# One consecutive block of 98 nodes per partition in the prologue of a graph-network kernel

## The chip, the cores and the metric

The kernel runs on one core of one Trainium2 chip. The metric is the device time of one execution in microseconds (us); the time before is 3852.42 us, the median of three runs (3849.85 to 3852.91).

## The reference

One layer of a message-passing network with 12,500 nodes of 128 features and 400,000 edges, which arrive sorted by their destination. All arithmetic is float32.

```python
h = jnp.maximum(_layernorm(x, axis=-1), 0.0)          # 12500 x 128, no scale or shift
m = relu(concat([h[src], h[dst], ea]) @ w1 + b1) @ w2 + b2      # 400000 x 128, ea has 32 columns
agg = segment_sum(m, dst, num_segments=12500)
gi = agg @ w_ih + b_ih ; gh = h @ w_hh + b_hh         # 3 gates of 128
r = sigmoid(i_r + h_r) ; z = sigmoid(i_z + h_z) ; n = tanh(i_n + r * h_n)
out = x + (1.0 - z) * n + z * h
```

## The kernel before

**Prologue.** The nodes are padded to 12,544 = 98 tiles of 128 (`NT`), and handled in 14 batches of 7 tiles (`NB`), alternately with parity 0 and 1. Node `n*128 + p` lies on partition `p` of tile `n`. For each batch SyncE loads x into `acc` (`load_x`, L313), VectorE takes the statistics (L805, L811), ScalarE the square root (`deviation`, L556), VectorE the reciprocal and the shift (`scales`, L820, L822). The normalising is shared: VectorE has tiles 0 and 1 (L830), GpSimd tiles 2 to 5 (L473, L475), ScalarE tile 6 (L565). TensorE transposes the seven tiles into PSUM (L1121). ScalarE applies the ReLU twice from the same PSUM: into `hT_batch` (L575), which TensorE reads as weights for the products with `w1_src` (L1130), and into `hT` (L576), the table of features by nodes that is kept for the whole kernel. ScalarE copies the products to `stage` (L583), and SyncE stores them in DRAM as `p_rows` (`store`, L319), row `n` of which is the product of node `n`. `stage`, the PSUM areas and `xn` have two buffers each, one for each parity. Each engine's program is in order; SyncE, TensorE, VectorE and ScalarE run the middle batches in a hardware loop of two batches a turn.

**Between.** SyncE loads the destinations in four parts into `dst_nat` (125 rows, L361), among the last stores. VectorE reduces them to the least and greatest node of each of the 125 chunks and two sets (L862, L863), and makes the window bases (`ranges_ready`) and the violations, which say whether the fast way is allowed. ScalarE makes `w2ih` and `b2ih` with TensorE (L619 to L623), then writes the bases to DRAM and reads them back, one copy for its registers and one on all partitions (L626 to L630), then zeroes two thirds of `acc` (L633); VectorE zeroes the rest (L878), makes `node_at` (L884), sets ones in `lhs` (L885), copies the iota to PSUM (L887) and makes the flag (L1103, L1104). Every engine waits for the flag before it goes on (`choose`, L303).

**Chunks.** The edges are handled in 125 chunks of 5 groups (`G`) of 5 tiles (`T`) of 128 edges. Per chunk GpSimd issues 24 indirect DMAs, each of which gathers 128 rows of `p_rows` (L501, `rows`). The 25th tile, tile 4 of group 3 (`PICKED`), is not gathered: for its 128 edges ScalarE (96) and VectorE (32) copy columns of `hT` into `picked` (L667, L938), a quarter in each of the steps 0 to 3, at node numbers that they read from `low` (`pick_act`, `pick_dve`), and TensorE multiplies (L1192). For the other groups TensorE computes the part from the destination and the edge features (L1187), VectorE adds it to the gathered rows (L947), ScalarE applies the ReLU (L673), and TensorE sums by destination with a one-hot matrix (L1207, `seg_ready`). The gathers of group `s` of the next chunk wait for `seg_ready[s]`. GpSimd starts the gathers of chunk 0 once all of `p_rows` is stored, before the flag. SyncE loads three groups ahead (`AHEAD`). For the picks it loads the node numbers of all chunks in two DMAs (L422), after the first three groups' loads and after the zeroes of `acc` were copied to `deg`.

Of the kernel before, what the change touches and what calls it, by code (L numbers as in the profile page):

```python
# [18 lines left out]
NB = 7  # L19
LOADS_AHEAD = 4  # L20
N_ZERO_DVE = N // 3

POOL_FROM = 2
ACT_FROM = 6
BATCHES = NT // NB
TAIL = N - (NT - 1) * P
# [8 lines left out]
CHUNKS = GROUPS // G  # L35
TILES = GROUPS * T
# [24 lines left out]
PICKS_DVE = (8, 8, 8, 8, 0)  # L61
PICKS_ACT = (24, 24, 24, 24, 0)
N_DVE, N_ACT = sum(PICKS_DVE), sum(PICKS_ACT)
assert N_DVE + N_ACT == P
# [12 lines left out]
def gnn_kernel(nc, x, src_cols, dst_cols, dst_rows, src_tiles, dst_tiles, ea_t, w1, b1, w2, b2, w_ih, b_ih, w_hh, b_hh, out):  # L77
# [7 lines left out]
    with ExitStack() as ctx:  # L85
# [6 lines left out]
        def sems(name, n):  # L92
# [5 lines left out]
        hT = sb("hT", [P, NPAD])  # L98
        low = sb("low", [P, NPAD])
# [17 lines left out]
        hT_batch = [low[:, at + k * NB * D:at + (k + 1) * NB * D] for k in range(2)]  # L117
        at += 2 * NB * D
# [5 lines left out]
        pick_dve = low[2 * ED:2 * ED + 1, 0:CHUNKS * N_DVE].bitcast(I32)  # L124
        pick_act = low[3 * ED:3 * ED + 1, 0:CHUNKS * N_ACT].bitcast(I32)
# [33 lines left out]
        zero_col = sb("zero_col", [P, 1])  # L159
# [52 lines left out]
        violT_ps = ps[0:1, 4096 - P:4096 - P + CHUNKS]  # L212
# [9 lines left out]
        pad_zeroed, x_tail_in = sem("pad_zeroed"), sem("x_tail_in")  # L222
# [3 lines left out]
        scaled, xn_dve_ready, xn_pool_ready, xn_act_ready, xT_ready, hT_ready, hT_kept = (sems(n, 2) for n in (  # L226
            "scaled", "xn_dve_ready", "xn_pool_ready", "xn_act_ready", "xT_ready", "hT_ready", "hT_kept"))
# [13 lines left out]
        pick_in, picked_dve, picked_act = (sem(n) for n in ("pick_in", "picked_dve", "picked_act"))  # L241
# [4 lines left out]
        g_src_in, g_dst_in = (sem(n) for n in ("g_src_in", "g_dst_in"))  # L246
        g_gathered = sems("g_gathered", 3)
# [62 lines left out]
        def _(sp):  # L310
            def load_x(k, par):
                xv = x[0:(NT - 1) * P, :].rearrange("(n p) f -> p n f", p=P)
                sp.dma_start(xt[:, bass.ds(k * NB, NB), :], xv[:, bass.ds(k * NB, NB), :]).then_inc(x_in[par], 16)  # L313

            pv = p_rows.rearrange("(n p) f -> p n f", p=P)
# [17 lines left out]
            sp.wait_ge(pad_zeroed, 1)  # L333
            sp.dma_start(xt[0:TAIL, NT - 1, :], x[(NT - 1) * P:N, :]).then_inc(x_tail_in, 16)
# [9 lines left out]
            k = BATCHES - 1  # L344
            sp.wait_ge(x_in[1], k // 2 * 16)
            xv = x[0:(NT - 1) * P, :].rearrange("(n p) f -> p n f", p=P)
# [8 lines left out]
            for s in range(G):  # L355
                load_indices(0, s)
# [1012 lines left out]
```

## Time and profile before

| | us |
|---|---|
| median of three runs | 3852.42 |
| the profiled execution's own time | 3851.74 |
| its span, first to last instruction | 3850.0 |
| GpSimd busy | 2863.6 (74%) |
| TensorE busy, matmul / weight load | 2907.2 (76%) / 2648.2 (69%) |
| VectorE busy | 2077.9 (54%) |
| ScalarE busy | 1921.0 (50%) |

The first 110 us are the prologue and the preparation of the chunks, the rest is the chunk loop, whose 40 slices on the page look alike. Issuing a DMA is not counted as busy, with the exception of GpSimd's indirect DMAs, which have rows of their own. The granted clock of TensorE is 1.0 of full speed in the prologue's loop, 0.5 between 64 and 100 us, and 0.74 over the whole span.

### The profile page before, as it was taken

The page shows a single profiled execution, that of the slowest core. Times are in us where ns is not written, and L with a number is a line of the kernel's source. Part 1 is how long each engine was busy: PE and PEld are TensorE (multiplying, and loading weights), DVE is VectorE, ACT ScalarE, POOL GpSimd, SP SyncE. Part 2 cuts the span into 40 slices and gives each one's busy share as a digit, 9 for nine tenths or more (in the row PEclk, how much of TensorE's full clock was granted, in tenths as well). Part 3 has the DMA queues.
Part 4 walks back from the last instruction along what each step waited for, and adds up shares of the span by engine and source line. Part 5 has one row for each costly group of instructions (what it writes and reads, how often), then busy time and mean ns, then how long its engine had stood idle before and what let it go on. Part 6 is the DMA issues. An engine that isn't in the chain of part 4 may idle for free.

```text
span 3850.0 us, 94115 instructions
## 1 busy us (share of the span) xinstructions
PE 2907.2 (76%) x16157; PEld 2648.2 (69%) x16157; DVE 2077.9 (54%) x8517; ACT 1921.0 (50%) x13700; POOL 2863.6 (74%) x3039
## 2 busy tenths in 40 slices
PE   4777777777678777877777777777777777787777
PEld 4677677667677766776766676677667767677776
DVE  5555555555555555555555555555555555555554
ACT  5545554455544455455544555445554455545553
POOL 5677777777777777777777777777777777777775
PEclk8777777877876677677777767777777776767776
DMA  7444444444444444444444444444444444444443
GB/s 187 111 113 111 111 111 111 115 111 111 111 112 112 111 111 111 112 111 111 111 111 112 111 111 111 111 114 112 111 111 111 112 111 111 111 112 111 111 111 80
DMA packets 439603, 433.42 MB, mean 113 GB/s; under 512 B 180055, under 2 KB 331062, under 8 KB 439572
## 3 DMA queue, kind: packets, MB, share of 16 engines
q0 software_dynamic: 96000, 196.80, 22.4%
q1 hardware_dynamic: 315254, 223.36, 19.5%
q10 hardware_dynamic: 28318, 12.94, 1.2%
q14 instruction: 23, 0.19, 0.0%
q8 instruction: 8, 0.13, 0.0%
HBM read 419.89 MB, written 12.82 MB: 112 GB/s over the span
## 4 chain that ended last, share of the span: by engine, by line
POOL 51%; issue 23%; PE 14%; DMA 3%; ACT 2%; ACTq 2%; DVE 1%; POOLq 1%; DVEq 0%; SPq 0%
POOL rows L501 51%; PE ps L1207 6%; DMA rows<-p_rows,idx 3%; ACT picked L667 2%; ACTq L658 2%; PE ps L1187 2%; PE ps L1222 2%; PE ps L1224 1%; PE ps L1221 1%; DVE rows L947 1%; PE ps L1192 1%; PE ps L1225 1%; POOLq L257 0%; POOLq L285 0%; DVE low L959 0%
## 5 line engine op out<-in xcount | busy, mean ns | idle before, releaser
L501 POOL DMA_INDIRECT rows<-p_rows,idx x3000 | 2833.2, 944 | 940.7 <-issue 897.8
L667 ACT COPY picked<-hT 128x1 f32 x12000 | 1181.4, 187 | 552.9 <-issue 552.9
L1187 PE MATMUL ps<-rhs,lhs 128*128 128x128 f32 x6250 | 1108.8, 341 | 72.5 <-DVE rows L947 67.5
L1207 PE MATMUL ps<-onehot,rows 128*128 128x95 f32 x6250 | 1074.4, 336 | 116.5 <-DVE low L959 116.5
L1207 PEld LDWEIGHTS ps<-onehot,rows 128*128 128x128 f32 x6250 | 1034.4, 253 | 153.7 <-issue 153.7
L947 DVE TENSOR_TENSOR rows<-rows,ps 128x640 f32<-128x640 f32 x625 | 495.7, 793 | 1153.9 <-DMA rows<-p_rows,idx 1146.9
L1187 PEld LDWEIGHTS ps<-rhs,lhs 128*128 128x128 f32 x6250 | 1020.8, 251 | 104.1 <-DVE rows L947 70.0
L673 ACT ACTIVATE rows<-rows 128x640 f32<-128x640 f32 x625 | 447.1, 715 | 1215.2 <-DVE rows L947 1213.8
L915 DVE TENSOR_SCALAR_CACHE_REDUCE lhs<-dst_row,node_at 95x640 f32<-95x640 int32 x625 | 543.3, 869 | 5.1 <-DMA dst_row<-in_dst_rows_dram 5.1
L906 DVE TENSOR_TENSOR onehot<-dst_rel,ps 128x475 f32<-128x475 f32 x625 | 401.0, 642 | 0.0
L938 DVE COPY picked<-hT 128x1 f32 x4000 | 349.8, 146 | 7.7 <-issue 7.7
L958 DVE TENSOR_TENSOR acc<-acc,ps 128x95 f32 x250 | 63.6, 254 | 511.9 <-PE ps L1210 441.7
L1192 PE MATMUL ps<-w_keep,picked 128*128 128x128 f32 x250 | 72.6, 381 | 339.8 <-ACT picked L667 339.8
L1229 PE MATMUL ps<-ident,upd 128*100 128x128 f32 x123 | 44.2, 359 | 336.9 <-DVE upd L978 336.9
L1192 PEld LDWEIGHTS ps<-w_keep,picked 128*128 128x128 f32 x250 | 46.8, 234 | 361.7 <-issue 361.7
L1222 PE MATMUL ps<-low,b2ih 1*128 (+1 forms) x738 | 267.4, 462 | 0.0
L1229 PEld LDWEIGHTS ps<-ident,upd 128*100 128x100 f32 x123 | 16.9, 137 | 363.4 <-DVE upd L978 362.9
L1221 PE MATMUL ps<-acc,w2ih 128*128 (+1 forms) x738 | 225.4, 407 | 0.0
L1222 PEld LDWEIGHTS ps<-low,b2ih 1*128 1x128 f32 x738 | 177.8, 298 | 62.8 <-issue 59.4
L1221 PEld LDWEIGHTS ps<-acc,w2ih 128*128 128x128 f32 x738 | 191.5, 317 | 0.0
L1224 PE MATMUL ps<-hT,whh_sb 128*128 (+1 forms) x492 | 180.7, 470 | 0.0
L1224 PEld LDWEIGHTS ps<-hT,whh_sb 128*128 128x128 f32 x492 | 120.7, 304 | 42.4 <-issue 40.6
(101 smaller groups left out, 1364.4 us busy)
## 6 DMA issues: line engine op xcount, KB each, us to landing
dst_row<-in_dst_rows_dram SPq DMA_DIRECT2D x625, 240.0 KB, 3.8
lhs<-in_ea_t_dram SPq DMA_DIRECT2D x625, 80.0 KB
rows<-p_rows,idx POOLq DMA_INDIRECT x3000
idx<-in_src_cols_dram SPq DMA_DIRECT2D x625, 2.5 KB
p_rows<-low SPq DMA_DIRECT2D x14, 448.0 KB, 4.4
x_fin<-in_x_dram ACTq DMA_DIRECT2D x123, 50.0 KB
out_dram<-out_fin ACTq DMA_DIRECT2D x123, 50.0 KB
acc<-in_x_dram SPq DMA_DIRECT2D x13, 448.0 KB, 4.5
```

Of the source, the lines that this page charges most:

```text
L501: pool.indirect_dma_start(out=rows[:, s, t, :], out_offset=None, in_=p_rows[:, :], in_offset=bass.IndirectOffsetOnAxis(ap=idx[:, s, t:t + ...
L667: last = nc.scalar.copy(picked[:, e:e + 1], hT[:, bass.ds(node, 1)])
L673: nc.scalar.activation(m, m, ACT.Relu).then_inc(message_ready[s], 1)
L906: nc.vector.tensor_tensor(onehot[:, ONEHOT_PLACE[s], :, 0:W], dst_rel[:, s * T:(s + 1) * T].unsqueeze(2).to_broadcast([P, T, W]), iota_ps. ...
L915: nc.vector.tensor_scalar(lhs[0:W, s, :, 0:P], dst_row[0:W, s, :].rearrange("w (t p) -> w t p", t=T), node_at[0:W, bass.ds(c * NSETS + SET ...
L938: last = nc.vector.tensor_copy(picked[:, e:e + 1], hT[:, bass.ds(node, 1)])
L947: nc.vector.tensor_tensor(r, r, pre_ps[s % 2][:, 0:k * D], ALU.add).then_inc(summed[s], 1)
L1187: last = nc.tensor.matmul(pre_ps[s % 2][:, t * D:(t + 1) * D], lhs[:, s, t, 0:P], rhs[:, k, :], start=True, stop=gathered)
L1207: done = nc.tensor.matmul(sg[:, 0:W], rows[:, s, t, :], onehot[:, ONEHOT_PLACE[s], t, 0:W], start=(first and t == 0), stop=(last and t == ...
L1221: nc.tensor.matmul(gate_ps[:, g, :], w2ih[:, cols], a, start=True, stop=False)
L1222: last = nc.tensor.matmul(gate_ps[:, g, :], b2ih[0:1, cols], d, start=False, stop=(g == 2))
L1224: nc.tensor.matmul(gate_ps[:, g, :], whh_sb[:, cols], h, start=False, stop=True)
```

## The change

- x is padded with zero rows to 12,544, and partition `p` now holds nodes `98*p` to `98*p + 97`: `load_x` and `store` move 7 consecutive rows of 512 bytes per partition, one piece of 3584 bytes, where there were seven pieces. The load of the last rows and the zeroing of the pad are gone.
- The transposed tile `n` now holds nodes `98*p + n`, so `hT`, still in node order, is written and read as weights at a step of 98 columns (`hT_nodes`). `hT_batch` and the ReLU into it are gone; the products read `hT_nodes`.
- The normalising is shared anew: VectorE 1 tile, GpSimd 4, ScalarE 2.
- TensorE's loop over the middle batches is unrolled.
- The destinations are loaded after the last store, whole rows in two parts (112 and 13 rows). VectorE zeroes all of `acc` before it reduces them. The flag is made directly after the violations, ahead of `w2ih` on TensorE and ahead of `node_at` on VectorE. ScalarE issues the DMAs of the bases before `w2T`, `w2ih` and `b2ih`. The ones in `lhs` are set at VectorE's very start.
- The node numbers of the picks are loaded for one step at a time (`load_picks`, four small DMAs per chunk, three steps ahead), and those of chunk 0 ahead of the wait for the zeroes of `acc`. ScalarE and VectorE wait for each (`wait_picks`), before the ReLU or the sum of the step.

```diff
-POOL_FROM = 2
-ACT_FROM = 6
+POOL_FROM = 1
+ACT_FROM = 5
+EVEN = CHUNKS // 16 * 16
+        hT_nodes = hT[:, :].rearrange("f (p n) -> f n p", n=NT)
-        hT_batch = [low[:, at + k * NB * D:at + (k + 1) * NB * D] for k in range(2)]
             def load_x(k, par):
-                xv = x[0:(NT - 1) * P, :].rearrange("(n p) f -> p n f", p=P)
+                xv = x.rearrange("(p n) f -> p n f", p=P)
-            pv = p_rows.rearrange("(n p) f -> p n f", p=P)
+            pv = p_rows.rearrange("(p n) f -> p n f", p=P)
...
-            store(turns + 0, 0)
-            load_ranges(0)
-            load_ranges(1)
             store(turns + 0, 1)
...
+            store(turns + 3, 1)
+
+            for first, last in ((0, EVEN), (EVEN, CHUNKS)):
+                sp.dma_start(dst_nat[first:last, :], dst_rows[first:last, :]).then_inc(dstn_in, 16)
+            sp.dma_start(w1_dst[:], w1[D:2 * D, :]).then_inc(weights_in, 16)
...
+            def load_picks(c, s):
+
+                wait(sp, picked_act, (c - 1) * len(TURN_PICKS) + s + 1)
+                wait(sp, picked_dve, (c - 1) * len(TURN_PICKS) + s + 1)
+                first, n = TURN_PICKS[s]
+                sp.dma_start(picks[:, first:first + n], nodes_of[bass.ds(c, 1), first:first + n]).then_inc(pick_in[s], 16)
...
                 for s in range(AHEAD):
                     load_group(0, s)
+                for s in range(len(TURN_PICKS)):
+                    load_picks(0, s)
...
-            def relu_tiles(i, par, first):
+            def relu_tiles(i, par):
                 act.wait_ge(xT_ready[par], i + 1)
-                if not first:
-                    act.wait_ge(p_ready[par], i)
-                nc.scalar.activation(hT_batch[par], xT_ps[par], ACT.Relu).then_inc(hT_ready[par], 1)
-                nc.scalar.activation(hT[:, bass.ds((i * 2 + par) * (NB * D), NB * D)], xT_ps[par], ACT.Relu).then_inc(hT_kept[par], 1)
+                nc.scalar.activation(hT_nodes[:, bass.ds((i * 2 + par) * NB, NB), :], xT_ps[par].rearrange("f (n p) -> f n p", p=P), ACT.Relu).then_inc(hT_kept[par], 1)
...
+            act.wait_ge(ranges_ready, 1)
+            act.dma_start(base_f_dram, base_f[0:CHUNKS, :]).then_inc(base_stored, 16)
+            act.dma_start(base_i_dram, base_n[0:CHUNKS, :]).then_inc(base_stored, 16)
             act.wait_ge(w2T_ready, 1)
             nc.scalar.copy(w2T, setup_ps[:, 0:D]).then_inc(w2T_copied, 1)
+            act.wait_ge(base_stored, 32)
...
-            nc.scalar.copy(acc[:, N_ZERO_DVE:N], zero_col[:].to_broadcast([P, N - N_ZERO_DVE])).then_inc(acc_zeroed, 1)
...
+            nc.vector.memset(acc[:, 0:N], 0.0).then_inc(acc_zeroed, 1)
...
+            dve.wait_ge(dstn_in, 32)
...
+            dve.wait_ge(violT_ready, 1)
+            link(nc.vector.tensor_reduce(flag_f[:], violT_ps, AX.X, ALU.max))
+            nc.vector.tensor_scalar(flag_i[:], flag_f[:], 0.0, None, ALU.is_gt).then_inc(flag_ready, 1)
+
             dve.wait_ge(base_bc_in, 16)
...
-                    last = nc.tensor.matmul(p_ps[par][:, t * D:(t + 1) * D], hT_batch[par][:, t * D:(t + 1) * D], w1_src,
+                    last = nc.tensor.matmul(p_ps[par][:, t * D:(t + 1) * D], hT_nodes[:, (i * 2 + par) * NB + t, :], w1_src,
                                             start=True, stop=True)
...
-            with pe.Fori(1, BATCHES // 2 - 1) as i:
+            for i in range(1, BATCHES // 2 - 1):
```

## Rows read from the trace of the kernel before

**Rows 1.** Costliest groups of the page: busy and mean ns; idle before, and releaser.

```profile
L501 POOL DMA_INDIRECT rows<-p_rows,idx x3000 | 2833.2, 944 | 940.7 <-issue 897.8
```

**Rows 2.** Timeline of GpSimd: start us, duration, what [idle before, releaser].

```profile
68.80 1.12 POOL L501 DMA_INDIRECT rows<-p_rows,idx  x1 [13.47 <-DMA p_rows<-low]
...
109.45 0.94 POOL L501 DMA_INDIRECT rows<-p_rows,idx  x1 [10.82 <-PE ps L1207]
...
118.14 0.94 POOL L501 DMA_INDIRECT rows<-p_rows,idx  x1 [2.75 <-PE ps L1207]
...
3828.22 0.94 POOL L501 DMA_INDIRECT rows<-p_rows,idx  x1 [0.30 <-issue]
```

**Rows 3.** Busy time by stretch; at the end granted clock, DMA share, GB/s.

```profile
30.00:40.00 10.00, 7.64 (x64) 7.19 (x65) 8.78 (x57) 9.78 (x17) 6.31 (x7) 1.00 0.95 265
...
60.00:64.00 4.00, 1.14 (x11) 0.94 (x9) 1.34 (x1) 0.81 (x2) 0.00 (x0) 0.94 0.96 289
```

**Rows 4.** Timeline, all engines, one batch of the prologue's loop.

```profile
27.48 1.45 DVE L805 BATCH_NORM_STATS2 stats<-acc 128x6 f32 x7 [0.38 <-issue]
27.72 0.91 ACT L576 ACTIVATE hT<-ps 128x896 f32 x1
27.96 1.64 PEld L1130 LDWEIGHTS ps<-low 128*128 128x128 f32 x14
...
28.43 1.04 POOL L475 TENSOR_TENSOR low<-low,shift 128x512 f32<-128x512 f32 x1
...
29.53 0.57 DVE L830 TENSOR_SCALAR low<-acc,mv,rstd 128x128 f32 x2
...
29.65 0.30 ACT L556 ACTIVATE std<-mv,eps_col 128x7 f32<-128x7 f32 x1 [0.22 <-DVE mv L811]
29.85 0.48 ACT L565 ACTIVATE low<-acc,shift,rstd 128x128 f32 x1
30.01 0.20 DVE L820 RECIPROCAL rstd<-std 128x7 f32<-128x7 f32 x1
...
30.58 0.95 PE L1121 MATMUL ps<-ident,low 128*128 128x128 f32 x7 [0.79 <-ACT low L565]
```

**Rows 5.** Timeline, the first and the last batches, and the ranges.

```profile
5.39 1.45 DVE L805 BATCH_NORM_STATS2 stats<-acc 128x6 f32<-128x128 f32 x7 [4.44 <-DMA acc<-in_x_dram]
...
14.81 1.45 DVE L805 BATCH_NORM_STATS2 stats<-acc 128x6 f32 x7 [0.62 <-DMA acc<-in_x_dram]
...
46.25 1.45 DVE L805 BATCH_NORM_STATS2 stats<-acc 128x6 f32<-128x128 f32 x7 [0.18 <-issue]
...
51.35 0.91 ACT L583 COPY low<-ps 128x896 f32<-128x896 f32 x1 [3.77 <-DMA p_rows<-low]
...
55.71 0.46 SPq L361 DMA_DIRECT2D low<-in_dst_rows_dram  x1
...
62.66 2.15 DVE L862 TENSOR_REDUCE gmin<-low 125x1 f32<-125x1920 int32 x1 [8.37 <-DMA low<-in_dst_rows_dram]
```

**Rows 6.** Timelines of VectorE, ScalarE and SyncE between ranges and first picks.

```profile
69.93 0.17 DVE L866 CAST base_n<-base_f 125x2 int32<-125x2 f32 x1
...
71.68 3.53 DVE L878 MEMSET acc<- 128x4166 f32 x1 [0.82 <-issue]
...
72.63 0.54 ACTq L626 DMA_DIRECT2D base_f_dram<-base_f  x1
...
76.79 0.22 ACTq L629 DMA_DIRECT2D low<-base_i_dram  x1
...
84.57 0.14 DVE L1104 TENSOR_SCALAR flag_i<-flag_f 1x1 int32<-1x1 f32 x1
...
86.07 0.27 ACT L647 COPY h_win<-hT 128x95 f32 x1 [1.51 <-issue]
...
90.35 1.89 SPq L422 DMA_DIRECT2D low<-in_src_tiles_dram  x2
...
98.89 2.32 ACT L667 COPY picked<-hT 128x1 f32 x24 [11.46 <-issue]
```

More of the change, by code:

```diff
@@ L60 @@
 PICKED = 3
[L61 to L64, printed above, removed]
+PICKS_DVE = ((0, 8), (32, 8), (64, 8), (96, 8))
+PICKS_ACT = ((8, 24), (40, 24), (72, 24), (104, 24))
+TURN_PICKS = tuple((d[0], d[1] + a[1]) for d, a in zip(PICKS_DVE, PICKS_ACT))
+assert sorted(e for first, n in PICKS_DVE + PICKS_ACT for e in range(first, first + n)) == list(range(P))
 IN_RANGE = "src holds node indices, 0 to N - 1"
@@ L355, in _ @@
-            for s in range(G):
-                load_indices(0, s)
-            part = G * GE // LOADS_AHEAD
-            def load_ranges(k):
-                sp.dma_start(dst_nat[:, k * part:(k + 1) * part], dst_rows[:, k * part:(k + 1) * part]).then_inc(dstn_in, 16)
             store(turns + 0, 0)
-            load_ranges(0)
-            load_ranges(1)
             store(turns + 0, 1)
+            store(turns + 1, 0)
+            store(turns + 1, 1)
+            store(turns + 2, 0)
+            store(turns + 2, 1)
@@ L403, in chunk @@
                         load_group(*ahead)
+                        if ahead[1] < len(TURN_PICKS) and not (isinstance(ahead[0], int) and ahead[0] == 0):
+                            load_picks(*ahead)
                     if s == 2 and exists((c + 1, 0)):
@@ L653, in copy_q, with wait_picks @@
                 nc.scalar.copy(rhs[0:W, k, :], q_ps).then_inc(rhs_ready[k], 1)
+            def wait_picks(c, s):
+                act.wait_ge(pick_in[s], c * 16 + 16)
+                wait(act, pre_ready[PICKED], c)
             def load_picks(c, s):
-                if isinstance(c, int) and c == 0:
-                    act.wait_ge(pick_in, 32)
+                first, n = PICKS_ACT[s]
                 _, nodes = nc.values_load_multi_w_load_instructions(
-                    pick_act[0:1, bass.ds(c * N_ACT + sum(PICKS_ACT[:s]), PICKS_ACT[s])], (mybir.EngineType.Activation,),
+                    picks[0:1, first:first + n], (mybir.EngineType.Activation,),
                     min_val=0, max_val=N - 1, skip_runtime_bounds_check_because=IN_RANGE)
@@ L663, in pick_columns @@
             def pick_columns(c, s, nodes):
-                wait(act, pre_ready[PICKED], c)
-                for e, node in enumerate(nodes, N_DVE + sum(PICKS_ACT[:s])):
+                for e, node in enumerate(nodes, PICKS_ACT[s][0]):
                     last = nc.scalar.copy(picked[:, e:e + 1], hT[:, bass.ds(node, 1)])
@@ L793, in _ @@
             nc.vector.memset(eps_col[:], EPS).then_inc(eps_set, 1)
+            nc.vector.memset(lhs[2 * ED:WB, :, :, 0:P], 1.0).then_inc(ones_set, 1)
             turn_reg = dve.alloc_register("turn")
@@ L934, in pick_columns @@
             def pick_columns(c, s, nodes):
-                wait(dve, pre_ready[PICKED], c)
-                for e, node in enumerate(nodes, sum(PICKS_DVE[:s])):
+                for e, node in enumerate(nodes, PICKS_DVE[s][0]):
                     last = nc.vector.tensor_copy(picked[:, e:e + 1], hT[:, bass.ds(node, 1)])
```

133 lines of the change are left out of this document (55 added, 78 removed).

## The prediction

> **What bounds the kernel now.** I began with the page's costliest groups, since no engine is busy all the time and the 40 slices are flat. The group to see is GpSimd's gather: 3000 of them at 944 ns, and between them 897.8 us of idle time that nothing ends but the issue itself [rows 1]. Both together are 3731 us of a span of 3850. The timeline of GpSimd says where it does wait: from 109.45 us on it has one wait more, 2.75 us ahead of the 30th gather at 118.14, and the 3000th starts at 3828.22 [rows 2]. That is 2970 intervals in 3710.1 us, 1.249 us each, so no wait of any size is left in them. The change leaves these 24 instructions per chunk as they are. The end is therefore set by when the 30th gather starts, plus 3710.1 us, plus the 21.8 us after the last start. Everything the change can win or lose by its prologue lies before 118.14 us.
>
> There GpSimd has three waits: it starts at 68.80 when the last store of p_rows has landed, runs chunk 0 back to back (24 gathers, 29.9 us, to 98.6), waits until 109.45 for the sums of group 0, and again for those of group 1 [rows 2]. So the store is not what decides: with the first gather 10 us earlier and nothing else changed, the wait at 109.45 is only longer. What decides is the chain that ends in the first sums. Followed back in the three engines' timelines it is: ScalarE's first picks at 98.89, from which ScalarE has no long idle time until the second sums; these waited for the node numbers, issued on SyncE at 90.35 to 92.24, behind three groups' loads; SyncE had waited for the flag, which VectorE made last, at 84.57, behind the ones in lhs and behind the bases' way through DRAM, whose two halves were issued at 72.63 and 76.79; and the bases came behind VectorE's reduction, from 62.66 to 70.10, which had waited for the destinations [rows 5, 6].
>
> **The change, part by part: the batches.** In the loop the turn of a batch takes 3.0 us, and 3.3 where the loop goes back; the row at 27.48 shows the 0.38 us [rows 4]. ScalarE looks like the bound (9.78 of 10 us busy [rows 3]), 3.1 us a turn of 3.15; the change takes one ReLU of 0.90 us from it, 0.8 of it not overlapped, and gives it one tile more, 0.3 us at a guess from the single tile's 0.48: 2.6 us. But VectorE is no looser: its statistics and their aggregation, ScalarE's square root from 29.65 to 29.95, and the reciprocal at 30.01 follow on one another. Its normalising, two tiles at 29.53, lies inside that gap [rows 4]. The tile that leaves VectorE saves it 0.05 us at most, and I take nothing. Thirteen turns lie between the statistics at 5.39 and those at 46.25; 0.6 us of it goes, a wait for x at 14.81. The last batch starts at 45.7 [rows 5].
>
> What the larger pieces do remove is the queue of the DMAs. They are 0.95 busy at 265 GB/s from 30 to 40 us [rows 3], x and p_rows being 12.8 MB in pieces of 512 bytes; at 51.35 ScalarE had waited 3.77 us for a store, and the square root of the last batch stood behind that copy [rows 5]. With that wait gone the last shift comes 2.9 us after the statistics' start, at 48.6; GpSimd's two operations of 1.04 and the transposes of 0.95 [rows 4] end at 51.9; the ReLU at 52.8, the products at 54.8, the copy, behind that of the other parity, at 55.8; the store is issued by 56.3. It takes 4 us to land, by the page's median of 4.4 and as the queue is shorter: 60.3. First gather at 60.3, chunk 0 done at 90.2. The ones in lhs, 3200 columns, take 2.7 us at the rate of the memset in rows 6; VectorE's first wait of 4.44 us for x hides them [rows 5], and without it they would cost their 2.7.
>
> **The zeroes and the ranges.** VectorE's memset took 3.53 us for 4166 columns [rows 6], so 12,500 take 10.6: from 51.9 to 62.5, and 62.9 with two small operations. The destinations, 1.6 MB, are issued behind the last store, at 56.5 to 57.5. At 300 GB/s (289 at a share of 0.96 in pieces of 512 bytes to 3200 [rows 3]) they and the rest of the store take 6.8 us, and with a completion of a microsecond they land at 64.2. So the memset is covered by 1.3 us, and the reduction starts 1.5 us later than at 62.66. That is the largest loss of the change. Bounds: 62.9, where the memset ends, and 84.7, if 1.6 MB took four times the 6.9 us that the last quarter took from its issue at 55.71 [rows 5]. I take 64.2, as that quarter shared the engines with stores and weights. The Trainium skill (DMA: Bandwidth & Descriptors, "Why a DMA increments its semaphore by 16 and not by 1") says a DMA is split over the largest number up to 16 that divides its slowest dimension: 5 engines for 125 rows, 16 for 112. It speaks for the early end; by it the upper bound is out, and the sum stays.
>
> **The chain behind.** Reduction and bases take 7.4 us as before: 71.6. ScalarE issues the bases' stores at once instead of after w2ih (72.63 against 70.10): 2.5 us are won. Its 4.2 us to 76.79 stay: 75.8. The loads follow; w2ih, TensorE's 1.4 us and b2ih now stand between, to 79.0, where ScalarE before had its zeroes. From the end of those to h_win it took 1.51 us: h_win at 80.5 against 86.07, 5.6 earlier [rows 6]. The rows' gap from there to the first picks, 12.8 us, was the wait for the node numbers. SyncE now gets the flag at about 73.5, loads three groups (0.5 us an issue) and the picks of chunk 0 by 79, so the numbers are there; what remains is q, 1.3 us, and the reading of registers, 1.7: picks at 83.5 against 98.89. The chain is 15.4 us shorter. The zeroes of acc are long done. From the first picks to the second sums nothing changes but the addresses of the node numbers. First sums at 94.05, 3.8 us behind the end of chunk 0, so GpSimd still waits for them, and both waits move by 15.4.
>
> **The chunk loop.** SyncE gets four issues more per chunk, 1.5 us, against 16 (three a group, and one) in 30 us. load_picks makes it wait for picks two steps old; behind it are queued the destinations and the next index loads. In the loop ScalarE's and VectorE's new waits stand ahead of the ReLU and the sum, but those already waited for the same pre_ready. A step is 6 us and the load is three steps ahead. I take nothing; what this costs if wrong is a rival. TensorE's unrolled loop I also take at nothing.
>
> **The step of 98 columns.** No row of before writes or reads many columns at such a step, so I bound it. Lower bound: nothing, or less for TensorE by no more than its own idle time. Upper bound: a multiple of the contiguous rows, 0.90 us for the ReLU and 1.64 for 14 weight loads, 0.117 each [rows 4]. ScalarE's turn becomes 2.6 us of 3.15, so the ReLU may cost 0.5 more for nothing; TensorE's is 0.95 + 1.64 and gaps, 2.7. I take nothing for both, nearest to the contiguous rows, since the number of elements is the same and ScalarE writes one at a time.
>
> **Sum.** 3850.0 - 15.4 = 3834.6 of span; with the 1.74 us around it 3836.3. The profiled execution is 0.7 below the median, so 3836.5.
>
> **Rivals.** *The step costs ScalarE double.* ReLU 1.6 instead of 0.8: turn 3.4, 0.3 over, 14 times: 4 us, 3840.5. For it: the busiest engine of the loop has it. Chance 0.12.
>
> *The strided weights make TensorE the bound, and the kernel slower.* It decides from where 14 turns grow by 15.4 us, a turn of 4.25, which is 0.23 us a weight load, 1.95 times now. At double the turn is 4.3 and the gain gone (3852, chance 0.05); at three times it is 6.0, 14 x 2.8 = 39 us more, 3876. For it: the weight loads are back to back now. Against it: they overlap with the matmuls, so part of a longer load may be hidden. Chance 0.07. The Trainium skill (Advanced Engine Details and Errata, "Memory Cachelines") says that SBUF has lines of 16 bytes and that an access to another line each time pays a penalty; at 392 bytes each column is such a one. It gives no figure; it is the rule against this change, and no run here shows it yet.
>
> *The preparation is shorter than I reckon.* Destinations at 62.9 and each handover faster; the floor is chunk 0's own end, 90.2, and no second wait: 109.45 - 90.2 + 2.45 = 21.7 us, 3830. Chance 0.11.
>
> *The destinations come as slowly as their last quarter did.* Then the chain is 5 us longer than before: 3857. Chance 0.02.
>
> *The picks' loads hold up the loop.* Only if a step's 12 us of lead is used up; 0.12 us in each of 125 chunks would take the gain: 3851. Chance 0.03.
>
> **How the numbers follow.** The forecast has 0.60, and lies within 4 us. About 0.2%, 7.7 us, is what a measurement can tell. Faster by more (below 3844.7): forecast, ScalarE and short preparation, 0.83, less 0.02 for their edges: 0.81. Slower: 0.09. Between: 0.10. Leaving out both TensorE cases' far part, the slow destinations and the edge below 3830, the range is 3829 to 3850.
>
> **What would show it.** The first gather near 60, the 25th near 94 after a wait of 4 us, the 30th near 102.7. No wait of ScalarE for a store. The ReLU at 0.90 us and 14 weight loads at 1.64. The reduction at 63 to 65, picks at 83 to 84. Gathers 1.249 apart. It is wrong if the turn of a batch grows beyond 3.3, if the destinations land after 66, or if GpSimd waits after its 30th gather.

## The result and the profile after

The changed kernel is slower: 3864.32 us, the median of eight runs (3861.01 to 3866.22), against 3851.48 of eight runs of the kernel before. The ratio is 1.0033, with a 95% interval of 1.0023 to 1.0042. The forecast was 3836.5 with a range of 3829 to 3850: wrong in its sign, and 28 us too low. The profiled execution took 3862.18 us, its span 3860.4 us.

The page's costliest group and GpSimd's timeline of the changed kernel, which answer to [rows 1, 2]:

```profile
L495 POOL DMA_INDIRECT rows<-p_rows,idx x3000 | 2834.7, 945 | 945.3 <-issue 910.2
```

```profile
77.78 1.12 POOL L495 DMA_INDIRECT rows<-p_rows,idx  x1 [16.63 <-DMA p_rows<-low]
...
121.31 0.94 POOL L495 DMA_INDIRECT rows<-p_rows,idx  x1 [13.69 <-issue]
...
128.97 0.94 POOL L495 DMA_INDIRECT rows<-p_rows,idx  x1 [1.72 <-PE ps L1205]
...
3840.25 0.94 POOL L495 DMA_INDIRECT rows<-p_rows,idx  x1 [0.30 <-issue]
```

The loop is nearly what it was: 2970 intervals in 3711.3 us, 1.250 us each, 1.2 us more in all than before. The loss is made before the 30th gather, which starts 10.83 us later (118.14 in [rows 2]); with the 1.2 us, and 1.6 less behind the last gather (20.15 us against 21.78), the span is 10.4 us longer. So the question is only what happened in the first 129 us.

Busy time by stretch of the changed kernel (PE, PEld, DVE, ACT, POOL; then granted clock, DMA share, GB/s), against [rows 3]:

```profile
30.00:40.00 10.00, 10.00 (x50) 10.00 (x51) 6.71 (x41) 8.90 (x11) 5.78 (x6) 1.00 0.75 240
...
60.00:70.00 10.00, 10.00 (x51) 10.00 (x50) 1.00 (x1) 7.23 (x8) 1.08 (x2) 1.00 0.24 96
...
90.00:100.00 10.00, 2.23 (x4) 0.72 (x4) 2.83 (x11) 0.53 (x2) 7.56 (x9) 0.50 0.76 43
100.00:110.00 10.00, 2.18 (x4) 0.48 (x4) 0.35 (x1) 1.21 (x4) 5.78 (x7) 0.50 0.98 202
```

Three things are to be seen. TensorE, 7.64 of 10 us busy before, has no idle time from 30 us until 70. The DMA share fell from 0.95 to 0.75, and from 40 to 70 us it is 0.24 to 0.34: the DMAs are no longer full, as forecast, and it was of no use. And between 90 and 110 us TensorE, VectorE and ScalarE stand nearly still, while GpSimd gathers.

One batch of the loop, all engines, against [rows 4]:

```profile
24.30 3.48 PEld L1128 LDWEIGHTS ps<-low,hT 128*128 128x128 f32 x14
...
25.62 1.85 ACT L566 ACTIVATE hT<-ps 128x896 f32 x1
...
27.57 0.93 PEld L1119 LDWEIGHTS ps<-ident,low 128*128 128x128 f32 x7
...
28.10 0.91 ACT L573 COPY low<-ps 128x896 f32<-128x896 f32 x1 [0.63 <-PE ps L1128]
28.47 1.78 PEld L1128 LDWEIGHTS ps<-low,hT 128*128 128x128 f32 x7
...
29.24 0.20 DVE L814 RECIPROCAL rstd<-std 128x7 f32<-128x7 f32 x1 [1.41 <-ACT std L550]
```

Fourteen weight loads take 3.48 us, 0.249 each, where they took 1.64, 0.117 each: 2.12 times. The one ReLU takes 1.85 us, as long as the two it replaced (0.90 and 0.91). The turn of a batch is 4.17 us (24.30 to 28.47), of which TensorE's own work is 3.48 and the transposes. ScalarE waits 0.63 us for the products, so it is not the bound, and VectorE's reciprocal waits 1.41 us for the square root that stands behind the ReLU and the copy in ScalarE's program.

The end of the prologue and the way of the bases, timelines of TensorE, ScalarE, VectorE and SyncE, against [rows 5, 6]:

```profile
66.09 6.97 PE L1128 MATMUL ps<-low,hT 128*128 128x128 f32 x28
69.00 10.47 DVE L854 MEMSET acc<- 128x12500 f32 x1 [9.94 <-issue]
74.40 1.17 SPq L360 DMA_DIRECT2D low<-in_dst_rows_dram  x2
84.39 2.15 DVE L864 TENSOR_REDUCE gmin<-low 125x1 f32<-125x1920 int32 x1 [4.74 <-DMA low<-in_dst_rows_dram]
91.63 0.17 DVE L868 CAST base_n<-base_f 125x2 int32<-125x2 f32 x1
91.83 0.55 ACTq L609 DMA_DIRECT2D base_f_dram<-base_f  x1
93.45 0.14 DVE L880 TENSOR_SCALAR flag_i<-flag_f 1x1 int32<-1x1 f32 x1
99.09 0.22 ACTq L616 DMA_DIRECT2D low<-base_i_dram  x1
108.01 0.27 ACT L636 COPY h_win<-hT 128x95 f32 x1 [5.80 <-issue]
109.44 0.35 DVE L884 TENSOR_SCALAR node_at<-base_bc,iota_p 128x250 f32<-128x250 f32 x1 [15.85 <-DMA base_bc<-base_f_dram]
110.92 2.32 ACT L657 COPY picked<-hT 128x1 f32 x24 [1.55 <-issue]
```

Against the forecast: destinations issued at 74.40 instead of 56.5 (17.9 late), landed at 84.39 instead of 64.2 (2.3 more), first picks at 110.92 instead of 83.5 (7.2 more; from the end of the bases at 91.80 to h_win at 108.01 it took 16.2 us, where 8.9 were reckoned). Together 27.4 us, and the 25th gather starts at 121.31 instead of 94.05, 27.26 late. Of this 25.8 us arrive in the span (3860.4 against 3834.6): the wait ahead of the 30th gather is 1.03 shorter than before, the loop 1.20 longer, the rest behind the last gather 1.63 shorter. The zeroing is covered by a wait of 4.74 us. There are thus three misses to explain: 17.9, 2.3 and 7.2 us.

### The profile page after: what moved, and what is told of

It is laid out like the page before. It is cut to its first block, busy times and chain, and to the rows that moved or that the text cites. A ratio compares the mean times of both kernels' runs of the same rounds, so it can differ in the third digit from the quotient of the medians.

```text
span 3860.4 us, 96654 instructions
## 1 busy us (share of the span) xinstructions
PE 2949.5 (76%) x16157; PEld 2685.5 (70%) x16157; DVE 2050.0 (53%) x8503; ACT 1912.6 (50%) x13699; POOL 2864.9 (74%) x3037
## 4 chain that ended last, share of the span: by engine, by line
POOL 49%; issue 22%; PE 17%; DMA 4%; ACT 3%; DVE 2%; ACTq 1%; POOLq 1%; DVEq 0%; SPq 0%
POOL rows L495 49%; PE ps L1205 7%; DMA rows<-p_rows,idx 3%; ACT picked L657 2%; PE ps L1185 2%; PE ps L1220 2%; PE ps L1222 1%; PE ps L1219 1%; ACTq L650 1%; PE ps L1128 1%; DVE rows L945 1%; ACT rows L663 1%; PE ps L1190 1%; PE ps L1223 1%; PE ps L1119 0%
## 5 line engine op out<-in xcount | busy, mean ns | idle before, releaser
L936 DVE COPY picked<-hT 128x1 f32 x4000 | 314.9, 145 | 0.5 <-issue 0.5
```

Of the source, the lines that this page charges most:

```text
L936: last = nc.vector.tensor_copy(picked[:, e:e + 1], hT[:, bass.ds(node, 1)])
```

## The experiments

Fourteen kernels gave a result (e4, an earlier form of e5, gave none). For two sets of them the chip was one on which the kernel before takes about 5000 us: 5064 us beside e1 to e3, 4997 us beside e9 to e12. There the picks of the loop are spaced by up to 1.4 us with no cause that the profile shows, and the times say little about the ordinary chip: on the one e1, e2 and e3 come out 1.9 to 2.1% slower than the kernel before beside them, on the other e9, e11 and e12 2.1 to 2.3% faster. From these sets only the traces of the prologue are used, whose times up to the ranges agree (reduction at 67.85 in e1 and at 67.95 in e6, the same kernel; at 84.30 in e9 and 84.39 in the changed kernel).

### The step of 98 columns

**e6 and e1: the change without the step.**

```diff
-        hT_nodes = hT[:, :].rearrange("f (p n) -> f n p", n=NT)
+        hT_nodes = hT[:, :].rearrange("f (n p) -> f n p", n=NT)
```

> The kernel of e1_packed_table once more, since its first runs and those of before beside it took over 5000 us, so that another bound in the chunk loop covered the prologue. If this chip runs the loop at the pace of GpSimd's gathers, the packed table takes 14 to 16 us off the kernel after: 1.000 of before, 0.998 to 1.001. Rival (the loss is not in the step): 1.003.

> The kernel after, but the prologue writes the kept table and reads it as weights contiguously; the table then holds the nodes in another order than picks and windows take them for (the output is not the reference's), x and products still move in 3584-byte pieces. Theory (the step of 98 columns doubles each weight load, 3.48 us for 14, and TensorE's turn is 4.17 us): 14 loads in 1.64 us, ReLU 0.90 us, turn back to 3.1 to 3.3, first gather at 62 to 64 instead of 77.8, and about 15 us off the end: 3848 to 3850. Rival (the turn grew by something else, the unrolled TensorE program or the new sharing of tiles): turn stays near 4.2 and the time near 3864.

Measured: e6 3847.42 us, ratio 0.9989 (0.9979 to 0.9999); e1 5163.09 against 5063.85 on its chip. Stretch and timeline of e6:

```profile
40.00:50.00 10.00, 7.61 (x64) 7.07 (x63) 8.15 (x52) 8.44 (x17) 6.52 (x7) 1.00 0.41 162
```

```profile
61.22 1.12 POOL L495 DMA_INDIRECT rows<-p_rows,idx  x1 [9.33 <-DMA p_rows<-low]
...
104.31 0.94 POOL L495 DMA_INDIRECT rows<-p_rows,idx  x1 [13.26 <-issue]
```

```profile
67.95 2.15 DVE L864 TENSOR_REDUCE gmin<-low 125x1 f32<-125x1920 int32 x1 [1.17 <-DMA low<-in_dst_rows_dram]
...
92.55 0.35 DVE L884 TENSOR_SCALAR node_at<-base_bc,iota_p 128x250 f32<-128x250 f32 x1 [15.43 <-DMA base_bc<-base_f_dram]
```

With the table packed TensorE is 7.61 of 10 us busy again, the reduction comes 16.4 us and the 25th gather 17.0 us earlier than in the changed kernel. The step costs 17 us here. Fourteen weight loads take 1.64 us again and the ReLU 0.90. But the rest of the change doesn't bring the 15.4 us of the forecast either: 5.1 us at the 25th gather (109.45 in [rows 2]), 4.3 on the median.

**e13: the kernel before with the step alone.**

```diff
-                nc.scalar.activation(hT_batch[par], xT_ps[par], ACT.Relu).then_inc(hT_ready[par], 1)
-                nc.scalar.activation(hT[:, bass.ds((i * 2 + par) * (NB * D), NB * D)], xT_ps[par], ACT.Relu).then_inc(hT_kept[par], 1)
+                nc.scalar.activation(hT_nodes[:, bass.ds((i * 2 + par) * NB, NB), :], xT_ps[par].rearrange("f (n p) -> f n p", p=P), ACT.Relu).then_inc(hT_kept[par], 1)
...
-                    last = nc.tensor.matmul(p_ps[par][:, t * D:(t + 1) * D], hT_batch[par][:, t * D:(t + 1) * D], w1_src,
+                    last = nc.tensor.matmul(p_ps[par][:, t * D:(t + 1) * D], hT_nodes[:, (i * 2 + par) * NB + t, :], w1_src,
```

> The kernel before with one part of the change alone: one ReLU, which writes the kept table at a step of 98 columns, and products that read it there (TensorE's loop unrolled for it). The pieces of 512 bytes, the ranges, the zeroes, the flag and the picks' loads stay as before. Nodes and table places don't match, so the picks take wrong columns; the work is the same. Theory (the step costs the gain on TensorE): turn of a batch 4.2 us, 14 weight loads 3.5 us, last transposes near 66, first gather near 77.5, the least nodes' reduction near 73 (before 62.66), first picks 8 to 12 us later than in the kernel before, time 8 to 12 us above it: ratio 1.002 to 1.003. Rival (the loop before was held by its DMA queue and hides a part of the step): first gather near 72 and under 5 us on the time, ratio below 1.0013. If the step isn't the cause, the ratio is below 1, since ScalarE has a ReLU less.

Measured: 3866.13 us against 3856.4, ratio 1.0025 (1.0016 to 1.0035). Stretch and timeline of e13:

```profile
30.00:40.00 10.00, 10.00 (x51) 10.00 (x51) 7.36 (x46) 7.70 (x9) 5.78 (x6) 1.00 0.85 233
```

```profile
77.98 1.12 POOL L502 DMA_INDIRECT rows<-p_rows,idx  x1 [16.05 <-DMA p_rows<-low]
...
127.17 0.94 POOL L502 DMA_INDIRECT rows<-p_rows,idx  x1 [2.10 <-PE ps L1207]
```

The step alone makes the kernel before 9.7 us slower by the medians, with the first gather 9.2 and the 30th 9.0 us later. The profiled execution, 3857.14 us, was the fastest of the ten: its span is only 5.4 us above that of the kernel before, since its loop took 2.4 us less and the end behind it 1.3 less. The times are the theory's; one part of it missed: the reduction came at 69.09, not near 73. With the step both kernels have their first gather at the same time, 77.98 here and 77.78 in the changed kernel; without it they have it at 68.80 and 61.22. So the price is 9.7 us here and 17 in the changed kernel because the loop before had its own losses at the end, among them the wait of 3.77 us for a store [rows 5], which is gone with the longer turn: prices of parts don't add when they share a bound.

**e2 and e11: which engine is the bound.** In e2 the products read the identity (contiguous) as weights, with the ReLU still at the step; in e11 the ReLU goes in the table's order, seven adjacent columns and then a jump, with the weights still at the step.

```diff
-hT_nodes[:, (i * 2 + par) * NB + t, :], w1_src
+ident[:], w1_src
```

```diff
-nc.scalar.activation(hT_nodes[:, bass.ds((i * 2 + par) * NB, NB), :], xT_ps[par].rearrange("f (n p) -> f n p", p=P), ACT.Relu)
+nc.scalar.activation(hT[:, :].rearrange("f (p n) -> f p n", n=NT)[:, :, bass.ds((i * 2 + par) * NB, NB)], xT_ps[par].rearrange("f (n p) -> f p n", p=P), ACT.Relu)
```

> The kernel after, but the products of the prologue take the identity, contiguous, as weights (so p_rows is wrong), while ScalarE still writes the table at the step of 98. It parts the two halves of the step. Theory: TensorE's turn falls to 2.7 us of work, and ScalarE with its ReLU at 1.85 us becomes the bound at 0.2 + 0.8 + 1.8 + 0.8 = 3.6 us a turn, so half of the loss comes back: first gather near 70, time 3855 to 3857. Rival (ScalarE's slow ReLU alone costs nothing): 3848 to 3850, like the packed table.

> The kernel after, but ScalarE's ReLU walks the table in its own order, seven columns side by side and then a jump of 98, and takes the strided side in PSUM. In e5_steps that took 0.98 us against 1.75 for the order of the kernel after. Theory (TensorE with its strided weight loads sets the turn of 4.17 us, ScalarE does not): ReLU near 0.95 us, turn and time as after, 3862 to 3866. Rival (ScalarE's ReLU is on the cycle with TensorE): the turn shrinks by up to 0.9 us and the time by up to 12 us.

Measured, by their traces: in e2 the ReLU is 1.84 us and ScalarE is busy without a gap, TensorE not:

```profile
30.00:40.00 10.00, 8.35 (x63) 7.15 (x63) 7.91 (x52) 10.00 (x15) 5.80 (x7) 1.00 0.79 269
...
66.70 1.12 POOL L495 DMA_INDIRECT rows<-p_rows,idx  x1 [12.06 <-DMA p_rows<-low]
```

The first gather comes at 66.70 (70 was expected), 5.6 us later than in e1 (61.14): that is what the longer ReLU costs by itself, near the 4 us of the prediction's rival. In e11 the ReLU is back at 0.98 us and ScalarE at 6.48 of 10, and nothing is won:

```profile
30.00:40.00 10.00, 10.00 (x51) 10.00 (x50) 6.58 (x41) 6.48 (x12) 5.77 (x6) 1.00 0.74 238
...
77.92 1.12 POOL L495 DMA_INDIRECT rows<-p_rows,idx  x1 [16.64 <-DMA p_rows<-low]
```

So both engines pay for the step, and TensorE's weight loads alone set the changed kernel's turn. Times on their chips: e2 5172.54, ratio 1.0207, where e1 had 1.0212; e11 4890.64, ratio 0.9787 (0.9753 to 0.9822).

**e5: the price by the size of the step.** Ahead of the prologue, 14 matmuls (28 weight loads) each with weights at a step of 1, 2, 3, 4, 5, 8, 16 and 25 floats, then ReLUs on ScalarE and copies on VectorE, out of PSUM, with the output at several steps.

```diff
+            for t in range(14):
+                last = nc.tensor.matmul(p_ps[0][:, 0:D], flat[:, 0:3*D:3], w1_src, start=True, stop=True)
...
+            nc.scalar.activation(flat[:, 0:3 * NB * D:3], p_ps[0], ACT.Relu).then_inc(bench_act, 1)
```

> The kernel after with a measurement at its start, after 100 products that warm TensorE: groups of 14 products with weights read at steps of 1, 2, 3, 4, 5, 8, 16 and 25 elements, then on ScalarE, and after it on VectorE, seven writes of a result each: 896 columns at steps of 1, 2 and 3, 768 columns at 4, seven tiles side by side written tile after tile at steps of 7 and of 25, and the same elements in the order of the destination, 7 next to each other and then a jump of 25. Theory A (each column that lies outside the line of the last one costs a fetch of its own): the 28 passes of a group go from 0.117 us each at step 1 to 0.25 at steps of 4 and more, with no change from 5 to 25. Theory B (the cost grows with the distance): 25 costs more than 8 and 4. ScalarE: 0.90 us at step 1, 1.85 at 7 and 25; 2 and 3 lie between if it is the line, and the order of the destination brings it back near 0.9. The time is some 50 us longer and tells nothing.

Timeline of e5, one row for each step of the weights in the order given above:

```profile
30.84 3.21 PEld L1150 LDWEIGHTS ps<-low,rows 128*128 128x128 f32 x28
...
33.97 3.38 PEld L1152 LDWEIGHTS ps<-low,rows 128*128 128x128 f32 x28
...
37.27 4.93 PEld L1154 LDWEIGHTS ps<-low,rows 128*128 128x128 f32 x28
...
42.11 6.62 PEld L1156 LDWEIGHTS ps<-low,rows 128*128 128x128 f32 x28
...
67.75 6.81 PEld L1164 LDWEIGHTS ps<-low,rows 128*128 128x128 f32 x28
```

From start to start, and divided by 28, a load takes 0.112 us at a step of 1, 0.118 at 2, 0.173 at 3 and 0.233 at 4; steps 5, 8, 16 and 25 gave 0.227, 0.238, 0.219 and 0.240, and 98 in the changed kernel 0.249. The price is nothing up to two floats, a half at three, double from four on, and it doesn't grow with the distance. ScalarE's ReLUs, for steps 1, 2, 3, 4 (768 columns), then tile after tile at 7 and at 25, and last in the order of the destination (seven adjacent, then a jump; here PSUM is read at a step of 128 floats):

```profile
76.36 0.92 ACT L590 ACTIVATE rows<-ps 128x896 f32<-128x896 f32 x1 [72.61 <-PE ps L1166]
77.31 0.95 ACT L592 ACTIVATE rows<-ps 128x896 f32<-128x896 f32 x1
78.29 1.35 ACT L594 ACTIVATE rows<-ps 128x896 f32<-128x896 f32 x1
79.67 1.51 ACT L596 ACTIVATE rows<-ps 128x768 f32<-128x768 f32 x1
81.22 1.76 ACT L598 ACTIVATE rows<-ps 128x896 f32<-128x896 f32 x1
83.01 1.75 ACT L600 ACTIVATE rows<-ps 128x896 f32<-128x896 f32 x1
84.80 0.98 ACT L602 ACTIVATE rows<-ps 128x896 f32<-128x896 f32 x1
```

VectorE's copies for the same seven cases took 1.09, 1.09, 1.33, 1.50, 1.75, 1.74 and 1.09 us. The time of the kernel, 3955.94 us, has these extra instructions in it. The Trainium skill (Advanced Engine Details and Errata, "Memory Cachelines") says of SBUF's 16-byte lines that at least two hits on a line are needed to absorb its latency. The rows agree with that reading: two floats of a line are used at a step of 2, one or two at 3, one from 4 on. The skill gives no price; here it is a factor of 2.1 for TensorE's weight loads, 1.9 for ScalarE (1.76 against 0.92 us) and 1.6 for VectorE (1.75 against 1.09). In time for each column the three come together: 0.9, 1.0 and 1.2 ns contiguous, and 1.7 to 2.0 ns for all of them from a step of four floats on.

### The pieces and the destinations

**e8 and e3: the change with pieces of 512 bytes** and the packed table.

```diff
-                xv = x.rearrange("(p n) f -> p n f", p=P)
+                xv = x.rearrange("(n p) f -> p n f", p=P)
...
-            pv = p_rows.rearrange("(p n) f -> p n f", p=P)
+            pv = p_rows.rearrange("(n p) f -> p n f", p=P)
```

> The kernel of e3_small_pieces once more, for the same reason. Theory: its first gather came 1.4 us behind that of the packed table (62.56 against 61.14), so it stands 1 to 4 us behind it here too: ratio 0.999 to 1.001 of before. Rival (the pieces of 3584 bytes carry a gain of their own): 5 us or more behind the packed table.

> The kernel after with the node order of before: x and products in pieces of 512 bytes, the table contiguous, one ReLU per batch, and all the rest of the change kept. Theory: the same turn as with the packed table, but the DMAs are 0.95 busy again, so the last stores land some us later than there: first gather 63 to 67, time 3848 to 3853. Rival (the larger pieces are what carries the gain): slower than the packed table by 5 us or more.

Measured: e8 3849.81 us, ratio 0.9996 (0.9986 to 1.0005), beside e6's 0.9989; e3 5159.58 on its chip, where e1 had 5163.09. In e8 the first gather comes at 62.16 (e6 61.22) and the 25th at 103.50 (104.31). ScalarE waits 0.93 us for a store, against 3.77 before. So the larger pieces are worth about a microsecond at the first gather and nothing at the 25th. The intervals of e6 and e8 overlap. From 30 to 40 us e8's DMAs are still 0.90 busy, at 261 GB/s, and its turn is no longer for it.

What took ScalarE's wait of 3.77 us away, then? Busy time by stretch, the kernel before around that wait, and below it e7 (described next), which has small pieces too and again loads the destinations among the last stores:

```profile
48.00:52.00 4.00, 0.79 (x8) 0.60 (x6) 0.87 (x8) 0.65 (x1) 0.43 (x1) 1.00 0.44 144
```

```profile
40.00:50.00 10.00, 7.94 (x67) 7.26 (x65) 8.24 (x54) 8.44 (x17) 6.26 (x6) 1.00 0.91 262
```

While ScalarE waited for its store, the DMAs were not full: 0.44 busy, and 0.33 to 0.36 at 108 to 132 GB/s in each microsecond from 49 to 53. The share is a mean over 16 engines, so a part of them, or all for a part of the time, stood idle. In e7 the share stays at 0.91, ScalarE waits 0.96 us, and the first gather comes at 62.17, as in e8. So neither the size of the pieces nor the place of the destinations made that wait. What differs is how a quarter of the destinations is moved, in one DMA of 125 rows before and in two of 112 and 13 rows in e7; e7 also has one ReLU a batch and loads the weights later. No run parts these, so that the single DMA of 125 rows held up the store is likely and not shown.

**e7: the destinations early.** As e8, with the destinations in four quarters among the last stores, and VectorE's zeroing behind the flag.

```diff
+            def load_ranges(k):
+                for first, last in ((0, EVEN), (EVEN, CHUNKS)):
+                    sp.dma_start(dst_nat[first:last, k * part:(k + 1) * part], dst_rows[first:last, k * part:(k + 1) * part]).then_inc(dstn_in, 16)
...
             store(turns + 0, 0)
+            load_ranges(0)
...
+            for par in range(2):
+                dve.wait_ge(xT_ready[par], BATCHES // 2)
+            nc.vector.memset(acc[:, 0:N], 0.0).then_inc(acc_zeroed, 1)
```

> Small pieces, contiguous table, one ReLU per batch, and the preparation turned round once more: the destinations are loaded in four quarters (each 112 and 13 rows) among the last stores, VectorE reduces them before it zeroes acc, and the zeroing stands behind the flag, where it covers the bases' way through DRAM. Theory (the chain to the first sums is what counts, and the last store is next): ranges ready near 60 instead of 92, first picks near 75, so GpSimd goes from chunk 0 (62 to 92) into chunk 1 with no wait or a short one; the 30th gather at 100 to 103 against 118.1 before: 15 to 18 us faster than before, ratio 0.995 to 0.996. Rival (the round trip of the bases lengthens by as much, since it then runs beside the stores): first sums after 100, ratio 0.998 or more.

Measured: 3837.24 us, ratio 0.9965 (0.995 to 0.9979), faster than both kernels. GpSimd's timeline of e7:

```profile
62.17 1.12 POOL L503 DMA_INDIRECT rows<-p_rows,idx  x1 [9.94 <-DMA p_rows<-low]
...
99.55 0.94 POOL L503 DMA_INDIRECT rows<-p_rows,idx  x1 [1.28 <-PE ps L1213]
...
3812.31 0.94 POOL L503 DMA_INDIRECT rows<-p_rows,idx  x1 [0.30 <-issue]
```

The reduction starts at 54.05 and the first picks at 81.16, so the sums are there when chunk 0 ends at 92.1, and the wait ahead of the 25th gather is gone. Of the chain, 1.28 us are left ahead of the 30th, 0.98 more than the usual 0.30; from here the first gather decides almost alone. The gain, 14.4 us, is a little less than the 15 to 18 expected. The 30th gather is 18.6 us earlier than before; 2.7 of that is lost in the loop (3712.8 us to the last start against 3710.1) and 2.4 behind it (24.2 against 21.8).

### The way of the bases

In the changed kernel it takes 17.6 us from the issue of the bases' stores (91.83) to node_at (109.44): 7.3 until the stores are done and the first load is issued (99.09), then 10.1 for the load to all partitions. In the kernel before it was 4.2 for the first part [rows 6] and 3.2 for that load, issued at 77.04, by VectorE's timeline:

```profile
80.22 0.35 DVE L884 TENSOR_SCALAR node_at<-base_bc,iota_p 128x250 f32<-128x250 f32 x1 [5.00 <-DMA base_bc<-base_f_dram]
```

What is new beside it is SyncE's loads for three groups, which follow the flag at 93.45, and more gathers under way.

**e9 and e14: SyncE's loads behind the bases; e10 and e15: the gathers behind the bases.** e9 and e14 are one edit, e10 and e15 the other; e14 and e15 ran on an ordinary chip.

```diff
             def fast():
+                sp.wait_ge(base_i_in, 16)
+                sp.wait_ge(base_bc_in, 16)
                 load_destinations(0)
```

```diff
+            pool.wait_ge(base_bc_in, 16)
             chunk(0)
```

> The kernel after, but SyncE starts its loads of the first groups and of the picks only once the bases have come back from DRAM. In the kernel after they start at 94.5 us, and the bases' store and load, issued at 91.8 and 99.1, take 6.7 and 10.1 us against 3.3 and 3.2 before. Theory (these loads are what delays the bases, since DMAs of SyncE and ScalarE share the engines): store and load back at 3.3 to 4 us each, bases on all partitions near 99.5, the first groups' loads behind them, first picks at 105 to 107 instead of 110.9, and 4 to 6 us off: 3859. Rival (the gathers delay them): round trip as long as after, and the loads now come behind it: 5 us or more slower than after, 3869.

> The kernel after, but GpSimd starts the gathers of chunk 0 only once the bases have come back. Theory (the loads of SyncE delay the bases): the round trip stays near 16 us, bases back at 108 to 109, gathers from there, so chunk 0 ends at 139 and chunk 1 follows with no wait: 30th gather near 147 against 129.0, 18 us slower than after. Rival (the gathers delay the bases): the round trip takes 6.5 us, bases back at 99, 30th gather near 137.

> The changed kernel; SyncE's loads for the chunks wait until the bases are back, the gathers run on. The same edit as in e9, here on a chip where the loop runs as in the profiles of before and after. Theory (gathers and loads together stretch the bases' way): from the issue of the bases' stores to node_at 8 to 10 us instead of 17.6, first picks all the same 108 to 112 us, since SyncE's loads start only then; time as after, within 3 us. Rival (the gathers alone stretch it): 15 us or more. Third (the loads alone): as the first here, and then e15 stays at 15 or more.

> The changed kernel; chunk 0's gathers wait until the bases are back, SyncE's loads run on. The same edit as in e10, on the same chip as e14. Theory (both together): bases' way 8 to 10 us, picks at 100 to 106; the gathers start near 101 instead of 77.78, so chunk 0 ends near 131, the 30th gather near 138, 9 us later than in the changed kernel: time 8 to 10 us above it. Rival (the loads alone stretch the way): 15 us or more, picks near 111, and time 17 above.

Measured on the ordinary chip (the kernel before: 3856.4): e14 3870.62 us, ratio 1.0037 (1.0024 to 1.0049), no better than the changed kernel; e15 3879.23, ratio 1.0058 (1.004 to 1.0077). VectorE's timeline of e14:

```profile
102.81 0.35 DVE L886 TENSOR_SCALAR node_at<-base_bc,iota_p 128x250 f32<-128x250 f32 x1 [9.22 <-DMA base_bc<-base_f_dram]
110.97 0.88 DVE L914 TENSOR_SCALAR_CACHE_REDUCE lhs<-dst_row,node_at 95x640 f32<-95x640 int32 x1 [7.81 <-DMA low<-in_src_tiles_dram]
```

and VectorE's of e15:

```profile
100.55 0.35 DVE L885 TENSOR_SCALAR node_at<-base_bc,iota_p 128x250 f32<-128x250 f32 x1 [6.59 <-DMA base_bc<-base_f_dram]
```

| from the issue of the stores | beside it | stores done | load back | in all |
|---|---|---|---|---|
| changed kernel | gathers and loads | 7.3 | 10.1 | 17.6 |
| e6 | gathers and loads | 6.8 | 10.1 | 17.2 |
| e8 | gathers and loads | 5.6 | 8.6 | 14.4 |
| e14 | gathers | 7.5 | 3.1 | 11.0 |
| kernel before | gathers, begun 3.8 us before | 4.2 | 3.2 | 7.6 |
| e13 | gathers, begun 3.8 us before | 4.6 | 3.1 | 7.9 |
| e15 | loads | 3.6 | 4.5 | 8.3 |
| e7 | gathers and loads, begun 0.7 and 2.7 us after | 8.5 | 6.9 | 15.7 |

The load back is slow only where the groups' loads (three times 240 and 80 KB, issued ahead of it) and the gathers are both there: 6.9 to 10.1 us, against 3.1 and 4.5 with one of them. So the theory of both together holds, though e14's 11.0 us in all lie above the 8 to 10 expected. The stores are another matter, which stays open: 3.6 us with no gathers and 4.2 to 8.5 beside them, and neither the loads nor how long the gathers have run puts these values in order. On their chip e9 took 8.9 us in all (5.7 and 3.0) and e10 8.8 (3.5 and 5.1; times 4901.5 us, ratio 0.9791, and 4891.32, one execution): the same answer. The theory of e9 and e10 (the loads alone) and its rival (the gathers alone) each fit one of the two and not both.

Neither helps. In e14 the wait only moves: node_at is ready at 102.81, but the next operation waits for the picks' node numbers until 110.97, and the first picks come at 112.77. In e15 the first picks come at 104.72, 6.2 us earlier, but chunk 0's gathers begin at 101.50. The expectation of 8 to 10 us over the changed kernel held as a ratio (1.0058 against 1.0033, 9.6 us).

**e12: e7 with e9's wait.** 

> The kernel of e7_early_ranges with the first groups' loads behind the bases, as in e9. There the bases' store took 7.6 us and their load 6.9, but VectorE's zeroing to 76.3 covers them, and GpSimd had only 1.3 us of waits left after chunk 0. Theory: the last 1.3 us at most, and the loads' own delay may take it back: 3836 to 3839, the same as e7_early_ranges (3837.2). Rival (the loads' delay now ends last): first picks after 84, 3840 or more.

Measured: 4888.58 us, ratio 0.9767 (0.9729 to 0.9805) on the chip of e9 to e11, where e11 had 0.9787: the intervals overlap. Its first gather comes at 62.05 and its first picks at 81.16, as in e7; what the wait adds to e7 it can't tell.

## Why the prediction was wrong

**The frame held.** The loop's interval went from 1.249 to 1.250 us, the chain to the first sums and not the store decides (in e15 it decides no longer, and in e7 hardly), and from the first picks to the 25th gather it takes 10.4 us, where the prediction had 10.55. The four new loads per chunk were taken at nothing; the loop is 1.2 us longer in the changed kernel and 1.7 in e6, and no run shows whether the loads are the reason. The ones in lhs and the zeroing were rightly taken at nothing, and the unrolled loop costs nothing that e6 shows. The reduction and the bases took 7.4 us (84.39 to 91.80), as reckoned.

**The step of 98 columns, 17 of the 27.4 us by e6.** This is the step that failed: "I take nothing for both, nearest to the contiguous rows, since the number of elements is the same and ScalarE writes one at a time". The measured factor is 2.12 for the weights (3.48 against 1.64 us) and 2.06 for the ReLU (1.85 against 0.90). It was named as a rival, with the right mechanism, and its arithmetic holds: double loads were to give a turn of 4.3 us, and 4.17 was measured. Its chance, 0.12 for all of TensorE's cases, was too small, and "they overlap with the matmuls, so part of a longer load may be hidden" has no row behind it. The rows spoke the other way: the loads of before fill 1.64 us back to back [rows 4], so a load that takes twice as long had nowhere to hide. The sum of the rival also left out that the products of the last two batches run after the last transposes: 6.97 us in the changed kernel, 3.29 in e6, another 3.7 us on the chain. The Trainium skill's rule (the same section as above) was quoted and set aside for want of a figure; with two elements a line needed, a step of 98 was a plain case of it.

**The bases' way, 7.2 us.** "Its 4.2 us to 76.79 stay" took a duration out of a stretch in which little else moved. The stores took 7.3 us, 3.1 more, for a reason that stays open. The change also brought the flag ahead of the bases' return, which released SyncE's loads just in front of the load back, and this took 10.1 us instead of 3.2; h_win came 8.9 us after its issue, where 4.7 were reckoned, which is the other 4.2. The prediction asked what an earlier flag lets start, but only for the picks, not for what it puts in front of the bases. e6 has this loss too, without the step; in e7 the zeroing covers most of it.

**The destinations, 2.3 us.** 7.7 us were reckoned from issue to landing, 10.0 were measured (10.1 in e6), inside the bounds given. The microsecond for the completion in that sum is shown by no run; the runs show only the whole.

**The gain itself was ascribed to the wrong edit.** The larger pieces were to remove the queue, and with it ScalarE's wait of 3.77 us for a store. e8 and e7 have that wait nearly removed without them, and while it lasted the DMAs were 0.44 busy: it was not the full queue of the loop, 0.95 busy, that the prediction took it for. And loading the destinations last, taken as a loss of 1.5 us, gives away much more: e7, with them early and the zeroing behind the flag, has its bases 13.9 us before e6.

Without the step the kernel would have come out at 0.9989 of before, which is 4.3 us and not 15.4. So one error was the sign's, and the others would still have made the forecast too good by 11 us.

## What to carry to other kernels

Where a layout for larger DMA pieces puts a stride into an operand that TensorE loads as weights, or that an engine writes, count the elements used of each 16 bytes first: with one float of four, a weight load took 2.1 times as long, and that was more than all the rest of the change won. Put the stride on the PSUM side instead, where ScalarE and VectorE paid next to nothing, and keep a packed copy for the weights as the kernel before did (the two together were not tried). When an edit brings a flag or a wait forward, list the transfers that it lets go and see which small, urgent one they now stand ahead of; and time a transfer by a row with the same neighbours. When an engine waits for a transfer, read the DMA share in just that stretch and not over the whole loop, before the pieces are made larger.

## What the runs showed of the hardware

The price of a step is a plateau, not a slope: 0.112, 0.118, 0.173, 0.233 us a weight load at 1, 2, 3, 4 floats, and 0.249 at 98. ScalarE and VectorE, which write, climb the same stairs as TensorE's loads, and all three end at 1.7 to 2.0 ns a column. Reading PSUM at a step of 128 floats while writing SBUF nearly in order cost ScalarE 0.98 us against 0.92, and VectorE nothing (1.09).

The DMA share tells neither the bandwidth nor how long a transfer waits: the engines were 0.76 busy at 43 GB/s from 90 to 100 us in the changed kernel, and 0.44 busy at 144 GB/s in the kernel before while ScalarE waited 3.77 us for a store. What stays open is why the bases' stores took 7.5 us in e14 and 4.6 in e13, both beside gathers only, what held up that store in the kernel before, and why two chips ran the loop at 5000 us.
